# A two-layer graph network kernel: the affine step of two quantisers put on ScalarE, and the final loads and stores of the last group put elsewhere in their queue

## The reference

```python
h = relu(layernorm(x))
xq = round(min(h / a1, 1) * 15)                       # features, 0..15
wq = round(clip((w - mean) / std / wa, -1, 1) * 7)
support = relu((xq @ wq) * (a1 / 15) * (wa / 7))
sq = round(min(support / a2, 1) * 15)                 # support, 0..15
x = x + (adj @ sq) * (a2 / 15)                        # scaling factor cancels
X = relu(layernorm(x)); Xf = Xa = X; Z = 0
for s in range(2):
    A = softmax(keep the top 0.9 of probability of (Xa@W1 @ W2 @ (Xa@W3).T))
    Xf = R @ Xf                                       # R: adj + I, rows summing to 1
    Xa = A @ Xa
    Z += Xf @ U1[s] + Xa @ U2[s]
x = x + layernorm(X + Z) * gamma + beta
```

## Time and profile before

| | us |
|---|---|
| median of 3 runs | 1296.33 |
| lowest, highest | 1292.09, 1300.24 |
| the profiled execution's own time | 1295.24 |
| its span | 1293.3 |
| mean granted PE clock, share of full | 0.953 |
| busy: PE, DVE, ACT, POOL | 1119.5, 1035.7, 439.4, 281.2 |

### The profile page before, as it was taken

The page is one execution under the profiler, slowest core; times in us unless marked ns, Lnnn a source line. Parts: engine busy times, 40 slices in busy tenths (PEclk is TensorE's granted clock), DMA queues, the critical chain, the costliest instruction groups (busy, mean ns, idle before and its releaser), DMA issues.

```text
span 1293.3 us, 16644 instructions
## 1 busy us (share of the span) xinstructions
PE 1119.5 (87%) x5402; PEld 518.1 (40%) x5402; DVE 1035.7 (80%) x2202; ACT 439.4 (34%) x836; POOL 281.2 (22%) x252
## 2 busy tenths in 40 slices
PE   0567999998999799799997999898999799789764
PEld 0223445454434344344443444343444344334321
DVE  7987777773599998899698006998997999999965
ACT  2544344444633033533432237540241251100000
POOL 6133333333122200101112010421111021011012
PEclk9888999999999899899998999898999899899887
DMA  7126466453334542341732513236844552743595
GB/s 244 65 69 220 166 205 209 168 199 118 95 117 153 143 89 43 90 82 42 147 82 66 96 51 130 90 117 243 193 91 136 134 115 90 187 114 107 148 266 156
DMA packets 190115, 170.62 MB, mean 132 GB/s; under 512 B 144656, under 2 KB 144656, under 8 KB 185936
## 3 DMA queue, kind: packets, MB, share of 16 engines
q1 hardware_dynamic: 190032, 169.66, 46.7%
HBM read 87.31 MB, written 48.76 MB: 105 GB/s over the span
## 4 chain that ended last, share of the span: by engine, by line
DVE 34%; PE 27%; issue 20%; POOL 7%; DMA 5%; ACT 5%; SPq 1%; POOLq 1%; DVEq 1%; ACTq 0%
PE RB L937 5%; DVE WS L1490 5%; DVE cand L1708 4%; PE UB L775 4%; PE AB L937 4%; DVE E L1721 3%; PE XB L775 3%; DVE WS L1705 3%; DVE WS L1713 3%; PE RB L939 3%; DVE g L1570 2%; PE AB L939 2%; DMA AD<-xu_d 2%; DVE E L1461 2%; DVE E L1720 2%
## 5 line engine op out<-in xcount | busy, mean ns | idle before, releaser
L1570 DVE TENSOR_REDUCE g<-E 128x1 f32<-128x2048 f32 x32 | 73.0, 2281 | 100.3 <-ACT E L1160 100.0
L1490 DVE SCALAR_TENSOR_TENSOR WS<-E,g 128x2048 bf16<-128x2048 f32 x48 | 119.6, 2535 | 0.4
L655 POOL TENSOR_TENSOR RT<-RT,AD 128x512 f32<-128x512 f32 x32 | 56.5, 1765 | 289.3 <-ACT RT L1220 289.2
L1708 DVE MAX8 cand<-WS 128x8 f32<-128x128 f32 x512 | 102.1, 276 | 1.1
L937 PE MATMUL AB<-VR,turns 128*128 128x512 f16 x256 | 66.3, 406 | 27.7 <-DMA turns<-E 27.7
L1713 DVE SCALAR_TENSOR_TENSOR WS<-E,g 128x2048 f32<-128x2048 f32 x33 | 80.9, 2450 | 0.9
L937 PE MATMUL RB<-VR,turns 128*128 128x512 f16 x256 | 64.2, 396 | 19.5 <-DMA turns<-E 19.5
L1721 DVE SCALAR_TENSOR_TENSOR E<-WS,E 128x2048 f16<-128x2048 f32 x32 | 79.1, 2472 | 1.1
L937 PE MATMUL RB<-XR,turns 128*128 128x512 f16 x256 | 63.8, 394 | 17.9 <-DMA turns<-E 17.9
L1197 ACT ACTIVATE E<-E,nmx 128x2048 f32<-128x2048 f32 x32 | 63.7, 1993 | 42.9 <-DVE nmx L1571 42.9
L672 POOL TENSOR_TENSOR XHL<-WF,XHL 128x512 f16<-128x512 f32 x16 | 22.1, 1383 | 250.0 <-ACT XHL L1245 250.0
(11 more groups left out here) (316 smaller groups left out, 2210.0 us busy)
## 6 DMA issues: line engine op xcount, KB each, us to landing
turns<-adj_parts SPq DMA_DIRECT2D x48, 512.0 KB, 3.8
E<-adjT SPq DMA_DIRECT2D x16, 1024.0 KB, 7.6
adj_parts<-turns SPq DMA_DIRECT2D x16, 1024.0 KB, 5.2
AH<-adj_parts SPq DMA_DIRECT2D x16, 512.0 KB, 4.1
z_d<-UO SPq DMA_DIRECT2D x28, 256.0 KB, 2.3
XR<-x SPq DMA_DIRECT2D x4, 1024.0 KB, 11.8
WS<-U SPq DMA_DIRECT2D x4, 1024.0 KB, 7.5
x_d<-WF SPq DMA_DIRECT2D x16, 256.0 KB, 2.0
```

The lines of the kernel that those rows point to most:

```text
L1490: return v.scalar_tensor_tensor(junk[t % 2], e, g4[:, k, t:t + 1], e, op, ALU.mult, accum_out=g4[:, F_, t:t + 1])
L1570: ct(v.tensor_reduce(row(A2)[:, t:t + 1], E[:, slot, :], AX.X, ALU.max))
L1708: i = v.max(cand[:, t, 8 * c:8 * c + 8], WS[:, c * PART:(c + 1) * PART])
```

## The change

**Quantisers.** POOL's four `ln_root` now stand ahead of `u_lo(0)`. DVE makes from each root a scale and a bias per row (`x_scale`, two instructions on 128x4), in between the statistics of the next batches. ACT then computes relu(scale * x + bias), four instructions of 128x512 per batch (`relu`); DVE's `quantise_x` keeps two passes (min and shift; shift back), `quantise_support` too, with `support_out` now a Relu with the whole scale in it; `support_rounded` is gone. `relu(3)` and `u_hi(0)` stand where `u_hi(1)` stood on ACT; `u_hi(1)` stands behind `adj_hi(1)`.

**Adjacency.** DVE's `adj_lo(0)`, `adj_sums(0)` and `own_block(0)` stand ahead of `quantise_support(0)`, and `wpk_parts` behind `quantise_x(3)`. SP's `adj_in(2)` stands ahead of `u_in(2)`.

**End.** Three buffer pairs for the batches, four buffers for tiles 12 to 15. The loads of `x1` for batches 0 and 1, and gamma, are issued at the start of group 2 of step 1; the loads of `z1` for all batches and `x1` of batch 2 at the start of group 3. All stores of the result stand behind the last `z_in`.

```diff
-        fin_y = [E[:, 2 * h, :].rearrange("p (t d) -> p t d", t=G) for h in range(2)]
-        fin_x = [E[:, 2 * h + 1, :].rearrange("p (t d) -> p t d", t=G) for h in range(2)]
+        fin_y = [E[:, b, :] for b in range(NG - 1)]
+        fin_x = [u[:, :, :, :].rearrange("p k h d -> p (k h d)").bitcast(F32) for u in (UW, UV)] + [E[:, NG - 1, :]]
...
-        gam, ends = WF, (UO, XF)
-        end_x = WS[:, :].rearrange("p (t d) -> p t d", t=G)
+        gam, ends = WF, (UO, XF, RT, AD)
...
             adj_in(1)
-            u_in(2)
             at_out(0, 0)
             adj_in(2)
+            u_in(2)
...
             def group_start(s, g):
+                if s == 1 and g == 2:
+                    sp.wait_ge(s_wl, T)
+                    fin_x_in(0)
+                    fin_x_in(1)
+                    sp.wait_ge(s_gb, 16)
+                    sp.dma_start(gam[:, :], gamma.partition_broadcast(P)).then_inc(s_gb, 16)
+                if s == 1 and g == NG - 1:
+                    for c in range(NC):
+                        sp.wait_ge(s_et[c], 16 * (T + G * (NG - 1)))
+                    fin_y_in(0)
+                    fin_y_in(1)
+                    fin_x_in(2)
...
                     if last and i == 0:
+                        sp.wait_ge(s_r, 2 * T)
                         end_in()
-                        fin_out(0, 1)
-                    if last and i == 1:
-                        fin_in(2)
-                        fin_out(1, 2)
...
+                if last:
+                    fin_out(0, 1)
+                    fin_out(1, 2)
+                    end_out(T - G, 3)
+                    fin_out(2, 4)
+                    for k in range(1, G):
+                        end_out(T - G + k, 4 + k)
...
-            u_lo(0)
             for b in range(NG):
                 ln_root(b)
+            u_lo(0)
             pool.wait_ge(s_sup, NG)
             u_lo(1)
...
-                a(to_round[:, t, :], (AB, RB)[t % 2][:, :], ACT.Copy, scale=sc[:, 22:23]).then_inc(s_mm1r, 1)
+                a(to_round[:, t, :], (AB, RB)[t % 2][:, :], ACT.Relu, scale=sc[:, 27:28]).then_inc(s_mm1r, 1)
+
+            def relu(b):
+                act.wait_ge(s_lnscale, b + 1)
+                for t in range(G * b, G * b + G):
+                    a(to_round[:, t, :], x_all[:, t, :], ACT.Relu, scale=ln_scale[:, 0, t:t + 1],
+                      bias=ln_scale[:, 1, t:t + 1]).then_inc(s_relu, 1)
...
             act.wait_ge(s_mm1, T + OPEN)
             adj_hi(1)
+            u_hi(1)
             u_hi(2)
             x_hi(0)
...
             def quantise_x(b):
-                for i in range(G):
-                    t = G * b + i
-                    (ch if i == G - 1 else ch.free)(v.tensor_scalar(
-                        to_round[:, t, :], x_all[:, t, :], mv[:, t, 0:1], rstd[:, t:t + 1], ALU.subtract, ALU.mult))
-                u = to_round[:, tiles, :]
-                ch(v.tensor_scalar(u, u, 0.0, sc[:, 20:21], ALU.max, ALU.mult))
-                ch(v.tensor_scalar(u, u, 1.0, 15.0, ALU.min, ALU.mult))
+                u = to_round[:, G * b:G * b + G, :]
+                dve.wait_ge(s_relu, G * b + G)
+                ch(v.tensor_scalar(u, u, 15.0, ROUND, ALU.min, ALU.add))
```

## The result

| | us |
|---|---|
| before, median of 4 runs (lowest, highest) | 1295.95 (1292.09, 1300.24) |
| after, median of 4 runs (lowest, highest) | 1249.61 (1248.6, 1251.4) |
| ratio, 95% interval | 0.9643 [0.9619, 0.9668] |
| after, the profiled execution and its span | 1250.26, 1248.3 |
| after, granted PE clock | 0.966 |

The account below looks back on a forecast made before the run. No engine was taken to bound the kernel alone; idle waits at start and end did. 1295.24 - 12.0 - 10.5 = 1272.7 against the profiled execution, 1273.5 by the median; range 1264 to 1285.

Parts of the forecast that it names:

- Start, to the support: Quantisers and support ahead of layer 0: terms sum to -5.6, so PE starts layer 0 at about 72.1 instead of 77.67.
- Start, to the loop: From layer 0's start to its steady loop: the whole start gains 12.0, bounds 6 to 16.
- The four terms -3.0 - 4.2 - 2.6 - 2.2: Layer 0's first tiles: earlier `U` chain 3.0, ACT's adjacency wait 4.2, PE's slow clock 2.6, part of the remaining excess 2.2.
- Middle: Groups 2 and 3 of step 1: early loads cost 0, up to 2 of PE's slack; no gain to be had.
- End: From tile 12 on: DVE's 10.83 wait for batch 2 goes, stores cost 0.3; gain 10.5, bounds 11 to 0.
- 1 and 2 (the `U` chain, the stores): `U` chain or early adjacency tile holds the start: 1279.5, chance 0.17. Stores hold the end: 1280, chance 0.12.
- 3 (table switches): ACT in the quantising stage: alternating Relu and Copy reloads tables, 33 longer, 1306; chance 0.02.
- the 0.04 for "other": Chance left for any outcome besides the forecast (0.65) and the three rivals.

Follow-up runs that it names:

- adj2_behind_u2: The changed kernel with the load of adjacency tile 2 moved back behind that of `U20`; 1247.43, ratio to before 0.9635.
- late_loads: The changed kernel, buffers and last stores kept, with gamma and the loads of batches 0 to 2 back in the last group; 1246.52, ratio to before 0.9623.
- old_rounding: The changed kernel with features rounded step by step as before, ACT in two steps, four more instructions per batch; 1278.98, ratio to before 0.9874.
- after_forced: The changed kernel made to run the tie-repair branch `in_order` for two tiles of step 1, group 1; 1271.27, ratio to before 0.9819.

## Why the prediction missed

- **Start, to the support: right, 0.6 too good.** Forecast 72.1, found 72.67. The first xq came at 36.55 (forecast 36.6), and the last support batch took 2.5 (forecast 2.5). Four Relus take 2.93, outside the bounds given for them (1.90 to 2.5, from a row of the same shape), not the 2.4 taken; that is 0.5 of the missing 0.6, and the figure of the Trainium skill ("ScalarE: Activation LUTs", Rules for kernel authors: about 0.3 plus 0.83 ns an element with a pointer bias) had said 2.9. The rule of the Trainium skill in the same section, VectorE and not ScalarE for relu, speaks against the move. With the Relus on ACT the stage ended 5.0 earlier, by the whole change of the start; no run has them on DVE in the new order.
- **Start, to the loop: right in size, in part by luck, and wrong in cause.** Forecast 12.0. Found 13.1 at the row for which it was made (148.27 before, 135.13 after), and 12.4 at x1 of tile 15. The four terms -3.0 - 4.2 - 2.6 - 2.2 came as 5.6, 4.4, 2.7 and 0.5 (PE's lead is 5.6 at the transposes of tile 0, 9.9 at the products by `U10`, 12.7 at tile 2's first product, 13.1 at the row of the forecast): the first was too small, the last too large. The `U` chain gave 5.6 instead of 3.0 (84.96 against 90.52) for two reasons. POOL's `u_lo(1)` took 4.07, the better of its two bounds. And the load of `U20` took 5.1 behind it (79.85 to 84.96), not the 6.8 read from the kernel before; that alone carries it past the forecast's better bound of 86.5. The 4.2 + 2.6 for PE's wait and slow clock did come, but `adj2_behind_u2` shows that the line they were put down to isn't needed. x1 of tile 0 came at 82.28 (82.2), by two errors that cancel: PE's product was done at 81.4, since its first 16 matmuls took 5.11 and not 6.10, and x1 then stood behind DVE's own low half, which ended at 82.0. The 57.9 "from x1 of tile 0" runs from PE's product at 90.34; from x1, at 89.45, it is 58.8.
- **Middle: the step that failed.** "Middle. ... cost 0 ... a gain isn't to be had" looked only at the new transfers, and those indeed cost nothing. It took for granted that an unedited stage repeats its work. That fails where the work depends on data and the change touches the data's last bits. The missing term is a branch worth 23.6 in the traces and 22 to 29 in the runs, and it turned 22.5 into 46.3. The profile's page named it: x33 beside x32. With the branch forced back in, the changed kernel takes 1271.27, near the 1273.5 forecast (1273.8, if 22.5 are taken from the median); with the old rounding kept, the new schedule gave 1278.98, in the forecast's range, of which 8.0 are its additional ACT instructions.
- **End: right.** Forecast 10.5, found 10.2 in the traces and 10.8 alone. DVE doesn't wait for batch 2. Measured from the last `rden`, POOL's add of tile 13 moved from 36.3 to 25.5, by the 10.8 of the forecast, and PE's last tile starts 20.9 before the end (20.5 before). The stores behind the last `Z` load cost nothing: the span ends 2.5 after DVE. `late_loads` shows that the loads' new places weren't part of it, as the forecast said of the 9.18 that PE waited for tile 13.
- **Rivals.** 1 and 2 (the `U` chain, the stores) didn't come. 3 (table switches) is excluded: one ACT_TABLE_LOAD, at 0.73. What did come was in none of them, only in the 0.04 for "other".

## What to carry to other kernels

Before costing the stages that a change doesn't edit, ask which of their instructions are conditional, and compare the counts of groups that ought to be equal: one count too many is a branch taken. A change of formula can switch such a branch even when the output stays as good, so a gain from it belongs to this input, not to the schedule. And when a wait has several conditions, look in the trace for the last one to be met: here a place in the queue was priced at 6.8, and with the place taken back nothing was lost (1247.43 against 1249.61).

## What the runs showed of the hardware

- **A branch costs idle time beside its instructions.** The first taken `in_order` began 5.38 after the read before it, all "issue", the second 1.37; with `old_rounding` 4.92 and 1.04. The body's rows sum to some 7.5 per tile, so of the 27.2 about 7 is idle time. In `after_forced` it lies elsewhere: 1.08 and 1.36 ahead of the two bodies, and 3.33 ahead of the repeated masking. The Trainium skill ("Runtime: NRT & Kernel Launch", Instruction fetch mechanics) says that a taken branch outside the fetched window stalls for its instructions; the rows agree with a stall, but don't show its cause.
- **VectorE was held while GpSimd ran.** The pass at 52.24 took 5.09 instead of 1.23 and ended at 57.33; POOL's low half had run from 51.49 to 56.24. The low half at 76.12 took 5.87 instead of 2.28; POOL ran from 75.78 to 79.85. Each ended 1.1 and 2.1 after POOL's instruction, about its own length alone:

```profile
51.49 4.75 POOL L592 TENSOR_TENSOR E<-WS,E 128x2048 f16<-128x2048 f32 x1 [18.25 <-ACT E L1053]
75.78 4.07 POOL L592 TENSOR_TENSOR E<-WS,E 128x2048 f16<-128x2048 f32 x1 [19.53 <-ACT E L1053]
```

It goes the other way round too. In the kernel before, DVE's low half had begun first (77.53, 2.28), and POOL's `u_lo(1)` at 77.69 took 6.06 instead of 4.06: 2.0 more, about what DVE still had to do. That fits what the Trainium skill ("SBUF — State Buffer", Who interferes with whom) calls an exclusive lock: one waits for the other, rather than both running slower. It cost little here: PE's product for x1 of tile 0 ended at 81.4, and x1 started at 82.28.

- **Scale and bias as columns.** Four 128x512 Relus from SBUF with both a scale and a bias per row took 2.93, or 2.92 in the row above, 0.73 each. With only one of the two (`old_rounding`, which takes them in two steps) four took 2.55, so the second costs about 0.1 an instruction. The plain row has 0.63.
